# A decoder block with routed experts: the second choice and the weights of the routing computed at the front of a step on VectorE, the positions counted ahead of the third scores on TensorE

## The reference

```
x = x + linear_attention(layernorm(x))        # 16 heads of 8; q, k, v by 128x128 weights; rope; elu + 1; causal, running sums; Wo
x = x + cross_attention(layernorm(x), ctx)    # q is the norm itself, k = v = ctx; 64 keys; softmax; mask
x = x + moe(layernorm(x))
moe(x): xn = norm(x) * ln_scale + ln_bias
        probs = softmax(xn @ gate_w.T)        # 8 experts
        the top 2, weights p / (p1 + p2 + 1e-5)
        shared swiglu(x) + sum over the two experts of weight * swiglu_e(x)   # inner size 256
```

## Time and profile before

| what | value |
|---|---|
| timed executions | 883.4, 883.92, 885.89 us |
| profiled execution, first to last instruction | 999.2 us (its span; the profile gives no other time of that execution) |
| TensorE busy | 830.2 us, 83% |
| VectorE busy | 661.5 us, 66% |
| ScalarE busy | 581.6 us, 58% |
| GpSimd busy | 550.5 us, 55% |
| chain that ended last | TensorE 64%, VectorE 16%, "issue" 11%, ScalarE 6% |
| mean granted TensorE clock | 0.911 |

### The profile page before, as it was taken

One profiled execution on the slowest core, in us unless ns is written; L12 is line 12 of the kernel. 1 busy time (PEld: TensorE's weight loads), 2 busy tenths in 40 slices (PEclk: granted clock), 3 DMA queues, 4 the chain that ended last, 5 costly groups with the idle time before them and its releaser, 6 DMA issues.

```text
span 999.2 us, 37214 instructions
## 1 busy us (share of the span) xinstructions
PE 830.2 (83%) x14611; PEld 626.2 (63%) x14611; DVE 661.5 (66%) x1800; ACT 581.6 (58%) x1185; POOL 550.5 (55%) x729
## 2 busy tenths in 40 slices
PE   3788997898898888898787677796989999999991
PEld 2456675666665665566564454685867877777780
DVE  1247786977766976887696396479455555556773
ACT  3568885786675785787685364352345555555450
POOL 5365456757656766666665454238125555555552
PEclk9799999998787998899898696799999999999995
DMA  9211110220210210210221101302212222225665
GB/s 243 50 46 45 46 46 24 62 51 24 62 50 24 62 51 25 63 54 28 57 54 50 32 13 57 104 17 57 54 33 75 77 74 76 78 71 168 195 186 162
DMA packets 96040, 68.56 MB, mean 69 GB/s; under 512 B 9680, under 2 KB 88027, under 8 KB 95872
## 3 DMA queue, kind: packets, MB, share of 16 engines
q1 hardware_dynamic: 84592, 47.95, 18.3%
q0 software_dynamic: 8640, 16.93, 4.8%
q10 hardware_dynamic: 2640, 1.31, 0.4%
HBM read 43.05 MB, written 24.02 MB: 67 GB/s over the span
## 4 chain that ended last, share of the span: by engine, by line
PE 64%; DVE 16%; issue 11%; ACT 6%; DMA 1%; POOL 1%; SPq 0%; another core or an unknown queue 0%; POOLq 0%; ACTq 0%; DVEq 0%
PE bank L875 8%; PE pair_x L857 7%; PE pair_x L573 6%; PE pair_x L664 5%; PE bank L681 5%; PE bank L610 4%; PE bank L490 3%; PE pair_y L857 3%; PE pair_x L740 2%; PE bank L843 2%; PE pair_y L740 2%; PE pair_y L573 2%; DVE Ex L1436 2%; PE bank L752 2%; PE pair_y L566 2%
## 5 line engine op out<-in xcount | busy, mean ns | idle before, releaser
L1333 POOL DMA_INDIRECT mixed<-f_y,f_x x142 | 138.8, 977 | 139.2 <-ACT f_y L1143 82.5
L1241 POOL DMA_INDIRECT routed<-c_row,c_idx x128 | 131.6, 1028 | 41.7 <-issue 41.7
L1202 POOL TENSOR_TENSOR Kblk<-ctxT,con 128x512 f32<-128x512 f32 x64 | 66.9, 1045 | 87.2 <-PE pair_y L573 45.8
L960 ACT ACTIVATE Am<-pair_x 128x1024 f32<-128x1024 f32 x64 | 65.3, 1020 | 73.0 <-PE pair_x L573 73.0
L610 PE MATMUL bank<-Vblk,Am 128*32 128x18 f32 x4096 | 68.9, 190 | 38.7 <-issue 35.4
L573 PE MATMUL pair_y<-Kblk,KQ 32*64 32x256 f32 x1024 | 100.0, 449 | 0.3 <-issue 0.2
L573 PE MATMUL pair_x<-Qblk,KQ 32*64 32x256 f32 x1024 | 97.1, 443 | 2.1 <-issue 2.0
L875 PEld LDWEIGHTS bank<-Qblk,Am 128*128 128x128 f32 x568 | 80.7, 191 | 24.7 <-issue 17.4
L610 PEld LDWEIGHTS bank<-Vblk,Am 128*32 128x32 f32 x4096 | 54.4, 112 | 62.1 <-issue 58.8
L875 PE MATMUL bank<-Qblk,Am 128*128 x568 | 91.7, 284 | 1.2 <-ACT f_y L1143 0.8
L995 ACT COPY ExT<-pair_x 128x1024 f32<-128x1024 f32 x64 | 64.5, 1008 | 48.0 <-PE pair_x L664 47.6
(11 more groups left out here) (210 smaller groups left out, 2142.4 us busy)
## 6 DMA issues: line engine op xcount, KB each, us to landing
f_x<-routed SPq DMA_DIRECT2D x142, 65.0 KB
ctxD<-in_ctx SPq DMA_DIRECT2D x32, 256.0 KB, 4.3
ctxP<-in_ctx SPq DMA_DIRECT2D x16, 256.0 KB, 2.8
maskB<-in_mask_BxS_if SPq DMA_DIRECT2D x16, 256.0 KB, 4.7
Cblk<-mixed SPq DMA_DIRECT2D x16, 256.0 KB
Kblk<-mixed SPq DMA_DIRECT2D x16, 256.0 KB
block_out<-X SPq DMA_DIRECT2D x11, 256.0 KB
mixed<-f_y,f_x POOLq DMA_INDIRECT x142
```

The costliest lines, as they stand in the source:

```text
L1202: return pool.tensor_tensor(dst[:, j, :, :, :], both.to_broadcast([P, 2, RH, T]), rows, ALU.mult)
L1241: pool.indirect_dma_start(routed[:, :], bass.IndirectOffsetOnAxis(ap=c_idx[:, par, t, n:n + 1], axis=0), c_row[:, par, t, n, :], None, bou ...
L1333: pool.indirect_dma_start(mixed[:, :], bass.IndirectOffsetOnAxis(ap=f_x[:, u, D + 1:D + 2].bitcast(I32), axis=0), f_y[:, u, :], None, boun ...
```

## The change

Three things move in the steps that have a group d, but not in the last one (s = 19), which stays as it was. No instruction is added or taken away.

- On VectorE `c_second` and `c_weights` stand at the front of the step, behind `c_first` and the second `a_divide`, ahead of `b_context`. Before, `c_second` stood behind `b_shift` part 1 and `c_weights` behind `b_shift` part 2.
- On VectorE `c_index` stands where `c_second` stood, ahead of `a_rotate`, `a_residual` and `b_statistics`. Before, it stood behind them.
- On TensorE `c_positions` stands behind `a_out`, ahead of the third part of the scores. Before, it stood behind those scores and `a_values` part 1, right ahead of `a_k_T`.

GpSimd's and ScalarE's orders stay the same.

```diff
@@ tensor, step
                 if on(h):
                     a_out(h, f)
+                if not s_is_last(s) and on(d):
+                    c_positions(d, h)
                 shared(s, 2)
                 scores(a, b, 2, par)
                 shared(s, 3)
                 if on(a):
                     a_values(a, 1, par)
-                if not s_is_last(s) and on(d):
-                    c_positions(d, h)
                 if on(f):
                     a_k_T(f, h, d)
@@ vector, step
                 if on(h):
                     a_divide(h, 1)
+                if not s_is_last(s) and on(d):
+                    c_second(d)
+                    c_weights(d, par)
...
                 if not s_is_last(s) and on(d):
-                    c_second(d)
+                    c_index(d, par)
                 if on(f):
                     a_rotate(f)
...
-                if not s_is_last(s) and on(d):
-                    c_index(d, par)
...
-                if not s_is_last(s) and on(d):
-                    c_weights(d, par)
```

## The result

Four timed executions of the changed kernel give a median of **940.89 us** (937.23 to 942.94) against 883.66 us (879.34 to 885.89) for four of the kernel before: ratio **1.0636**, 95% interval 1.0589 to 1.0683. The sign was forecast, the size was not: +57 us instead of +8, and 35 us above the range.

What follows compares the result with a forecast made beforehand. VectorE was taken to bound a timed step, 29.2 us of work in 30.1. Seven fast-front steps at +1.68 less four slow ones at 1.0 gave +7.8 on 883.9, 892 us; range 887 to 902, 8 in 10 872 to 906.

Steps and rivals of the forecast that it cites:

- The sign: Whole kernel: slower, by +7.8 us to 892; chance of slower 0.61, same 0.13, faster 0.26.
- The period before: A timed step of the kernel before, fast front: 23.14 + 6.96 = 30.1 us, against 36.3 in the trace.
- fast front: Step start with TensorE at full clock, 6.96 us to `b_divide`; the change makes such a step 31.78 us, +1.68.
- slow one: Step start at half clock, TensorE's path 9.85 us, hiding VectorE's 9.61; the change takes the step from 33.0 to 32.0, -1.0.
- about 100 of the 115 us as gaps: First trace's excess over timed runs: about 100 us gaps absent when timed, the rest clock.
- The middle of the step: From `b_divide`, with `b_shift` part 0 done, to the end of `b_shift` part 3: 23.14 us before, 22.17 with the change.
- The wait at `c_pos`: VectorE at the early `c_index`: a new wait of 1.87 us for TensorE's counts when VectorE is late.
- The 1.06 us of TensorE: TensorE's wait for `c_read` at `a_k_T`: removed, but taken as 0 gained, since `a_q_T` then waits for ScalarE.
- The front: From the end of `b_shift` part 3 to `b_divide`: VectorE needs 9.61 us with the change, where TensorE's path is 6.96.
- TensorE's clock falls: Rival, chance 0.09: `a_project` waits for `b_context`, some 3 us new idle, later matmuls 1.5 us longer; 919 us.
- The serial path: Front: `a_project` queues behind late `b_context`; VectorE's 9.61 us sum was used, TensorE's path being 6.96.
- behind the 11 steps: Steps from 15 on, lacking `a_rotate` and `a_feature`: counted as nothing, between -4 and +4 us.

Runs made afterwards that it cites:

- e1: The kernel before, unchanged, profiled a second time: 888.47 us, span 886.7 us, period 30.97 us.
- after: The changed kernel as profiled, all three moves in, against the kernel before: median 940.89 us, ratio 1.0636; span 935.4 us.
- e9: Separate small kernel without the block: one VectorE instruction beside five GpSimd products. With two SBUF inputs it took 1.16 and 4.82 us, alone 0.19.
- e5: The changed kernel with `c_second` and `c_weights` moved behind `b_context`, ahead of `b_shift` part 0: 979.7 us, ratio 1.1044 to the kernel before.
- e7: The kernel before with `c_second` behind `b_shift` part 0, early counts, and `c_index` between `a_residual` and `b_statistics`: 917.13 us, ratio 1.0342.
- e4: The changed kernel with 26 filler transposes on TensorE ahead of `a_project`'s wait in the 11 steps: 928.07 us, ratio 1.0466 to the kernel before.
- e6: The kernel before with only `b_context` moved, behind `b_shift` part 0: 901.11 us, ratio 1.0198.
- e3: The changed kernel with `c_weights` back at its old place: 888.48 us, ratio 1.0034 to the kernel before.

## Why the prediction was right in sign and wrong in size

**The period before: right.** 23.14 + 6.96 = 30.1 was forecast out of an execution with 36.3; e1 has 31.01, in parts 23.11 and 7.90. The mix was taken too slow: "7 of the 11 steps with a fast front and 4 with a slow one", where e1 has 9 and 2. With those the forecast's own sum is 9 x 1.68 - 2 x 1.0 = +13.1 us, 897.

The reason given for the odd execution was not right. It took "about 100 of the 115 us as gaps" that the timed runs don't have, from the shares of "issue" in the chain. e1 has such shares too, over the same four stretches 13.0, 10.4, 12.7 and 20.4%, which is 119 us to 114. This is its stretch from 98 to 527 us:

```profile
by line: issue 10.4%; PE pair_x L573 8.0%; PE pair_x L664 7.1%; PE bank L681 6.4%; DVE Ex L1436 6.0%; DVE mx L1432 5.7%; PE bank L490 4.9%; ACT Am L960 4.5%; PE bank L610 3.6%; PE pair_y L566 2.6%; DVE rot L1370 2.4%; PE bank L703 1.9%; PE
```

Of the 112.5 us between the spans 999.2 and 886.7 TensorE's busy time has 65.1 (830.2 and 765.1, mean granted clock 0.911 and 0.953) and its idle time 47.4. The period came right since it was added up from durations and one path, and not from those shares.

**The middle of the step: right, by nearly equal terms.** The wait at `c_pos` was forecast at 1.87 us and is 1.97 in the step shown, 18.4 us in 11, 1.67 on average. From `b_divide` to `c_index` it is 289.08 - 282.15 = 6.93 (6.76 forecast). The 1.06 us of TensorE was taken as 0, since `xfT` would stop it: it did, 8.3 us in 9. One wait was missed: VectorE stands 1.58 us at `b_divide` (298.01) for the values, so it reaches `a_feature` after 17.06 us and not 15.93, and makes up for part of it later. From `b_divide` to the next `c_softmax` 22.17 was forecast and 22.46 measured on average, 0.65 less than in e1 where 0.97 less was forecast.

**The front: the step that failed.** 9.61 us was forecast from the end of `b_shift` part 3 (the start of `c_softmax`) to `b_divide`, as a sum of VectorE's own durations; 12.44 is measured, 2.83 more, in 11 steps 31 us. It has three terms, and the sum had none of them:

- *`c_second` and `c_weights` don't keep their durations.* "`b_context` ends 7.2 us after `b_shift` part 3"; it ends at 8.50, 1.3 us later. Two of the four groups that grew, first of after and then of e1 (busy us, mean ns of one):

```profile
L1514 DVE TENSOR_TENSOR c_row<-c_best,c_m 128x8 f32<-128x8 f32 x16 | 15.9, 993 | 0.6
...
L1486 DVE TENSOR_TENSOR c_hit<-c_t,c_min 128x32 f32<-128x32 f32 x16 | 7.5, 470 | 0.5
```

```profile
L1486 DVE TENSOR_TENSOR c_hit<-c_t,c_min 128x32 f32<-128x32 f32 x16 | 5.1, 318 | 0.6
...
L1514 DVE TENSOR_TENSOR c_row<-c_best,c_m 128x8 f32<-128x8 f32 x16 | 3.7, 233 | 0.6
```

 Behind them L1487 grew from 7.6 to 9.0 us and L1512 from 3.0 to 6.2. Together (15.9 + 9.0 + 7.5 + 6.2) - (7.6 + 5.1 + 3.7 + 3.0) = 19.2 us over 16 groups, 1.2 a step. All four have both inputs in SBUF. For `c_hit` (L1486) and `c_row` the step above shows GpSimd's block beside them; for the other two it is inferred. e9 shows the collision by itself, without scatters, and e5 and e7 its size where more of GpSimd's work lies there. `c_row` in e5 and `c_hit` in e7 began to stand 0.33 and 0.41 us ahead of the products, while GpSimd issued a scatter; whether that holds VectorE too was not run. The Trainium skill (GPSIMD Engine Reference, Key points) says that GpSimd shares its SBUF interfaces with VectorE, in contention with VectorE's instructions that have two inputs in SBUF or run in a mode of two ports; e9 agrees, with 1.16 and 4.82 us against 0.19. I had not weighed this rule, though it speaks against a chain of such instructions in this very place.

- *The clock.* `a_project` takes 3.02 us on average for 1.89 in e1 and 1.98 in e4. From the end of `b_context` to `b_divide` are 12.44 - 8.50 = 3.94 us, and in e4, at full clock, 11.40 - 8.49 = 2.91, so 1.03 us a step lie on the path; e4 gives back 12.8 to 15 us when TensorE is kept busy. The prediction had this as a rival, "TensorE's clock falls", with a chance of 0.09 and 919 us, deciding when `a_project` waits longer than TensorE waits now. It does in each step, 37.0 / 11 = 3.4 us; the "some 3 us of new idle" was right. The evidence against, that waits of 1.06 us bring no fall, says nothing of a wait three times as long. The Trainium skill (TensorE: Matmul & The Clock Gate, HAM oscillation) describes a wait between bursts of matmuls after which each burst starts at half clock; the window with 0.54 behind 4.44 us of wait agrees. Three steps, behind 0.82, 2.56 and 2.89 us, kept the full clock.

- *The serial path.* 9.61 was the sum of VectorE's own work, `b_shift` (2.39) being the last of it. But `a_project` can't start before `b_context`, and the values follow it. So `b_divide` comes 2.91 us behind `b_context` even at full clock (e4), 0.5 more than 2.39. The prediction named this dependence and then took the larger of two sums where the second begins inside the first. e6 shows that lateness alone costs 1.5 us a step for 2.0 us.

1.3 + 1.03 + 0.5 = 2.83, as measured. With them the forecast's period of a step with a fast front, 31.78, becomes 31.78 + 2.83 + 0.29 = 34.90, where 0.29 is the middle (22.46 for 22.17). Against 31.01 before that is 3.89 us a step, 42.8 in 11. These are the measured parts put in for the forecast ones, so their sum must come out; what the runs bear out by themselves is the collision (e9), the clock (e4) and the price of a late `b_context` (e6).

**The sign came right for its reason.** The forecast had the front longer by 2.65 us (9.61 for 6.96) and the rest of the step shorter by 0.97; measured are 4.54 (12.44 for 7.90) and 0.65. e3 keeps the wait at `c_pos` and loses 0.3%, so the loss is the front's, and three fifths of its 4.54 us were not in the sum.

**What stays open:** the 6.8 us between the spans behind the 11 steps, counted as between -4 and +4, lie above that and were not taken apart. Whether the 26 transposes of e4 cost something of their own, beside the clock that they keep up, can't be told: its period is 1.07 us shorter, and `a_project` alone is 1.04 shorter. Why the clock fell in eight of the 11 steps and not in three isn't shown.

## What to carry to other kernels

Before small instructions are moved into an engine's idle time, ask which instruction queues behind them, who waits for that one, and add the path from there: here the idle at `b_context` was 0.8 us a step, the chain put ahead of it took 3.55 us by its old durations and more in its new place, and TensorE, which had not waited there, waited 3.4. A small instruction of VectorE with two inputs in SBUF has no fixed price; it has to be kept away from the stretches where GpSimd works without a break. And a profiled execution whose span is far from the timed times should be profiled again, or read for durations only, before its idle is counted as room.

## What the runs showed of the hardware

- VectorE's small instruction beside GpSimd's run: 0.19 us alone; 1.16 or 4.82 with two inputs in SBUF, 1.15 with one input and a constant; 0.19 with an operand in PSUM or as a reduction (e9). In the kernel up to 5.49 us shown for 0.2 (e7). It can stand until the run ends (4.82 us, four products), not only until the instruction beside it does (1.16 us).
- TensorE's eight matmuls of `a_project` took 1.99 us behind waits of 0.82, 2.56 and 2.89 us, and 2.57 to 3.78 us, at a granted clock of 0.75 to 0.50, behind eight waits of 2.29 to 4.44 (after). With the filler and waits of at most 1.67 us they took 1.89 or 1.99 in all 11 steps (e4).
- One execution of the same kernel had a span of 999.2 us and another one of 886.7, with a mean granted clock of 0.911 and 0.953, and TensorE busy for 830.2 and 765.1 us. The share of "issue" in the chain doesn't tell the two apart (114 and 119 us).
